# Fewer semaphore waits, and the shifted rows by a second TensorE transpose, in a Mamba layer with six local-attention layers

## The reference, cut to what matters

```python
# Mamba, forward and flipped, on the normalised x
h = h * exp(dt * A) + (dt * u) * B;  y = (h @ C + u * D) * silu(z)

# each of the 6 layers; shift_tokens moves half of the features one token on
q, k, v = split(shift_tokens(x) @ Wqkv)          # 16 heads of 64
q, k = rotary(l2norm(q) * qs), rotary(l2norm(k) * ks)
k2, v2 = [previous window of 32, own window of 32]
out = softmax(mask(q @ k2.T * 8)) @ v2
x = out @ Wo + x
x = (a * gelu(gate)) @ W2 + b2 + x                # a, gate = layernorm(shift_tokens(x)) @ W1 + b1
```

## Time and profile before

| what | us |
|---|---|
| median of 2 runs | 3917.16 |
| lowest and highest of them | 3916.18, 3918.15 |
| the profiled execution, its own time | 3923.24 |
| its span, first to last instruction | 3921.5 |
| outside the span | 1.7 |

### The profile page before, as it was taken

The page is one execution under the profiler, slowest core; times in us unless marked ns, Lnnn a source line. Parts: engine busy times, 40 slices in busy tenths (PEclk is TensorE's granted clock), DMA queues, the critical chain, the costliest instruction groups (busy, mean ns, idle before and its releaser), DMA issues.

```text
span 3921.5 us, 115027 instructions
## 1 busy us (share of the span) xinstructions
PE 3716.7 (95%) x45104; PEld 2578.1 (66%) x45104; DVE 3307.3 (84%) x3327; ACT 3035.4 (77%) x7250; POOL 3178.6 (81%) x2370
## 2 busy tenths in 40 slices
PE   7999999988799999999999999999999999999997
PEld 2444444433377777777777777777777777777775
DVE  2999999999688887888878887888878888788885
ACT  7776667666488887888878887888878887888885
POOL 2787778877688888888888888888888888888883
PEclk8999999999899999999999999999999999999999
DMA  1122222222100000000000000000000000000001
GB/s 60 71 81 76 76 74 73 81 73 84 43 21 7 20 7 6 21 7 20 7 10 18 7 20 6 11 17 7 21 6 10 18 7 20 7 11 6 7 7 47
DMA packets 62307, 115.01 MB, mean 29 GB/s; under 512 B 10820, under 2 KB 37320, under 8 KB 61648
## 3 DMA queue, kind: packets, MB, share of 16 engines
q1 hardware_dynamic: 61776, 107.66, 8.3%
HBM read 90.32 MB, written 4.72 MB: 24 GB/s over the span
## 4 chain that ended last, share of the span: by engine, by line
PE 66%; issue 3%; ACT 2%; POOL 1%; DVE 0%; POOLq 0%; ACTq 0%; DVEq 0%
PE ps L1199 17%; PE ps L1127 13%; PE ps L1188 9%; PE ps L1138 8%; PE ps L1175 6%; PE ps L1224 5%; PE ps L1237 3%; PE ps L1160 2%; PE ps L1206 1%; PE ps L1212 1%; PE ps L1146 1%; POOL resid L1604 1%; POOL resid L1626 0%; ACT prob L1329 0%; ACT mixed L1338 0%
## 5 line engine op out<-in xcount | busy, mean ns | idle before, releaser
L1604 POOL TENSOR_TENSOR resid<-resid,sq 128x1024 f32<-128x1024 f32 x384 | 910.3, 2376 | 2.1 <-DVE sq L1459 2.1
L696 POOL TENSOR_TENSOR read<-state,c_row 128x1024 f32<-128x1024 f32 x256 | 646.2, 2540 | 178.7 <-DVE state L658 99.4
L1626 POOL TENSOR_TENSOR resid<-resid,rnorm 128x1024 f32<-128x1024 f32 x384 | 725.0, 1904 | 17.8
L1199 PEld LDWEIGHTS ps<-mixed,w_vo 128*128 128x128 f32 x6144 | 710.9, 193 | 26.7 <-issue 18.6
L1199 PE MATMUL ps<-mixed,w_vo 128*128 128x128 f32 x6144 | 720.2, 276 | 3.2 <-ACT mixed L1338 3.2
L1127 PE MATMUL ps<-w_qk,xs_parts 128*128 128x512 f32 x2304 | 635.6, 412 | 37.4 <-issue 19.4
L1329 ACT ACTIVATE prob<-ps,stat 128x64 f32<-128x64 f32 x3072 | 650.8, 382 | 0.7 <-DVE stat L1479 0.5
L1459 DVE TENSOR_TENSOR sq<-ps,rope_l 128x1024 f32<-128x1024 f32 x384 | 462.5, 1205 | 103.9 <-ACT sq L1291 103.7
L1472 DVE TENSOR_TENSOR resid<-ps,rope_l 128x1024 f32<-128x1024 f32 x384 | 464.9, 1211 | 82.5 <-ACT sq L1291 75.2
L1291 ACT ACTIVATE sq<-ps 128x1024 f32<-128x1024 f32 x384 | 395.6, 1030 | 154.2 <-PE ps L1127 121.4
L1127 PEld LDWEIGHTS ps<-w_qk,xs_parts 128*128 128x128 f32 x2304 | 414.0, 192 | 152.5 <-issue 74.1
(11 more groups left out here) (149 smaller groups left out, 6038.1 us busy)
## 6 DMA issues: line engine op xcount, KB each, us to landing
c_row<-c_rows SPq DMA_DIRECT2D x128, 512.0 KB, 3.6
rows_back<-rows SPq DMA_DIRECT2D x192, 48.0 KB, 1.9
w_stage<-w_qk_hbm SPq DMA_DIRECT2D x12, 512.0 KB, 4.6
vo_stage<-w_v_hbm SPq DMA_DIRECT2D x6, 512.0 KB, 4.0
vo_stage<-w_o_hbm SPq DMA_DIRECT2D x6, 512.0 KB, 5.0
rows_back<-rows SPq DMA_DIRECT2D x192, 16.0 KB, 1.8
xn<-x_hbm SPq DMA_DIRECT2D x4, 512.0 KB, 5.7
kept<-resid SPq DMA_DIRECT2D x8, 256.0 KB, 4.2
```

What stands on the lines that cost most here:

```text
L696: pool.tensor_tensor(read[:, h, g % 2, :], state[:, h, g % 2, :], c_row[:, g % C_AHEAD, :], ALU.mult).then_inc(done[f"rd{h}"], 1)
L1199: last = pe.matmul(bank[:, 0:P], w_vo[:, l % 2, head_at(place_h), :], mixed[:, odd, place_h, :], start=place_h == 0, stop=place_h == HEADS ...
L1604: pool.tensor_tensor(qk[:, tile % 2, cols], qk[:, tile % 2, cols], sq[:, 1 + part, :], ALU.add).then_inc(done[f"rotated{part}"], 1)
L1626: pool.tensor_tensor(heads, heads, norms, ALU.mult).then_inc(done[f"normed{part}"], 1)
```

## The change

Two things are changed.

1. `after` sorts the stages asked for by the engine that makes them (`places` numbers the stages of each engine's order). Of each engine's only the latest is waited for, and only when the waiting engine hasn't already waited for that stage or a later one of that engine (`latest`, with the record `met`). Stages with a negative number are left out. Bank waits and stage waits of a stage go through one such call (`freed_by`). `add_ff` and `in_norm` are now stages like others (`x_of`), so that `x_low` isn't waited for any more. In `mamba` the waits for `cd` and `cst` (transfers) stay as they were, and are asked for first.
2. `rows_back` and its two transfers a tile are gone. `row_turn` makes two transposes, one of the tile's 128 columns of xa and one of the 128 columns that begin 32 before, into the two quarters of one bank; `copy_rows` copies 128x256 instead of 128x128 into `rows[:, tile % 2, back or own, :]`. `mix` takes both from there.

```diff
+def places(orders):
+    return {stage: (side, n) for side, order in enumerate(orders) for n, stage in enumerate(order)}
+
+def latest(met, eng, stages, places):
+    asked = {}
+    for side, n, stage in sorted((*places[stage], stage) for stage in stages if stage[1] >= 0):
+        asked[side] = n, stage
+    asked = {side: x for side, x in asked.items() if x[0] > met.get((eng.engine, side), -1)}
+    met.update({(eng.engine, side): n for side, (n, _) in asked.items()})
+    return [stage for _, stage in asked.values()]

# mamba
             for name, k in producers:
-                if k >= 0:
+                if k >= 0 and name in ("cd", "cst"):
                     eng.wait_ge(c_spread[k % C_AHEAD] if name == "cd" else done[name], COUNT[name, k])
+            for stage in latest(met, eng, [x for x in producers if x[0] not in ("cd", "cst")], stands):
+                eng.wait_ge(done[stage[0]], COUNT[stage])

# transformer
-    rows = sb("rows", [P, 2, P])
-    rows_back = sb("rows_back", [P, 2, P])
+    rows = sb("rows", [P, 2, 2, P])

     def after(eng, *producers):
-        for name, k in producers:
-            eng.wait_ge(done[name], k + 1)
+        for name, k in latest(met, eng, producers, stands):
+            eng.wait_ge(done[name], k + 1 + CHUNKS * int(name == "add_ff"))

             for tile in range(ALL_TILES):
                 l, t, odd = place(tile)
-                shift_rows(tile)
+                after(sp, ("copy_rows", tile))

             def row_turn(tile):
                 l, t, odd = place(tile)
-                ff_added(pe, CHUNKS * l + t // CHUNK_TILES)
-                bank = turn_free("row_turn", tile)
-                pe.transpose(bank[:, 0:P], shifted(xa, t * P, P), ident[:, :]).then_inc(done["row_turn"], 1)
+                bank = turn_free("row_turn", tile, x_of(CHUNKS * l + t // CHUNK_TILES))
+                first = column(t * P)
+                for back in (WINDOW, 0):
+                    to = bank[:, 0:P] if back else bank[:, P:2 * P]
+                    last = pe.transpose(to, xa[:, first - back:first - back + P], ident[:, :])
+                last.then_inc(done["row_turn"], 1)

             def mix(tile):
-                after(pe, ("turn_probs", tile), ("copy_rows", tile))
-                shifted_back(pe, tile)
-                banks = [turn_free("mix", tile, w) for w in range(WINDOWS)]
-                for own, of in enumerate((rows_back, rows)):
+                after(pe, ("turn_probs", tile), ("copy_rows", tile), *[x for w in range(WINDOWS) for x in freed_by("mix", tile, w)])
+                banks = [turn_bank("mix", tile, w) for w in range(WINDOWS)]
+                for own in range(2):

             def copy_rows(tile):
-                after(act, ("row_turn", tile))
-                if tile >= 2:
-                    after(act, ("mix", tile - 2))
-                    shifted_back(act, tile - 1)
-                act.copy(rows[:, tile % 2, :], turn_bank("row_turn", tile)[:, 0:P]).then_inc(done["copy_rows"], 1)
+                after(act, ("row_turn", tile), ("mix", tile - 2))
+                act.copy(rows[:, tile % 2, :, :], turn_bank("row_turn", tile)[:, 0:2 * P].rearrange(
+                    "p (b n) -> p b n", b=2)).then_inc(done["copy_rows"], 1)
```

More of the change, by code:

```diff
@@ L204, in mamba @@
         y_ps = [ps[:, 4 + 2 * h:6 + 2 * h, :] for h in range(HALVES)]
+        met, stands = {}, places((PE_SEQ, ACT_SEQ, DVE_SEQ, POOL_SEQ))
         COUNT, done = {}, {}
@@ L970, in transformer, with x_of @@
     KEPT = 16 * CHUNKS
+    met, stands = {}, places((PE_SEQ, ACT_SEQ, DVE_SEQ, POOL_SEQ))
+    done |= {"in_norm": x_ready, "add_ff": x_ready}
     def after(eng, *producers):
-        for name, k in producers:
-            eng.wait_ge(done[name], k + 1)
-    def ff_added(eng, chunk):
-        eng.wait_ge(x_low, chunk + 1)
-        eng.wait_ge(x_ready, chunk + 1)
-    def shifted_back(eng, tile):
-        eng.wait_ge(rows_shifted[tile % 2], 32 * (tile // 2 + 1))
+        for name, k in latest(met, eng, producers, stands):
+            eng.wait_ge(done[name], k + 1 + CHUNKS * int(name == "add_ff"))
+    def x_of(chunk):
+        return ("in_norm", chunk) if chunk < CHUNKS else ("add_ff", chunk - CHUNKS)
     def indexed(name, f, n):
@@ L1028, in load_w2 @@
                 if l >= 2:
-                    ff_added(sp, CHUNKS * l - 1)
+                    after(sp, x_of(CHUNKS * l - 1))
                 sp.dma_start(w2[:, l % 2], hbm["w2"][l]).then_inc(w2_loaded, 16)
                 sp.dma_start(lp[:, l % 2], hbm["lp"][l]).then_inc(w2_loaded, 16)
-            def shift_rows(tile):
-                l, t, odd = place(tile)
-                after(sp, ("copy_rows", tile))
-                if tile >= 2:
-                    after(sp, ("mix", tile - 2))
-                before = (tile - 1 if t % SEQ_TILES else tile) % 2
-                sp.dma_start(rows_back[WINDOW:P, odd], rows[0:P - WINDOW, odd]).then_inc(rows_shifted[odd], 16)
-                sp.dma_start(rows_back[0:WINDOW, odd], rows[P - WINDOW:P, before]).then_inc(rows_shifted[odd], 16)
             load_heads(0)
@@ L1096, in turn_free @@
                 elif last:
-                    after(pe, (TURN_READERS[last[0]], last[1]))
-                return turn_bank(name, k, i)
+                    return [(TURN_READERS[last[0]], last[1])]
+                return []
+            def turn_free(name, k, *producers):
+                after(pe, *producers, *freed_by(name, k))
+                return turn_bank(name, k)
             def fold(two):
@@ L1103, in stage @@
                     pe.wait_ge(wvo_loaded, 32 * l + 32)
-                    banks = [turn_free(f"fold{two}", l, odd) for odd in range(2)]
+                    after(pe, *freed_by(f"fold{two}", l, 0), *freed_by(f"fold{two}", l, 1))
+                    banks = [turn_bank(f"fold{two}", l, odd) for odd in range(2)]
                     for h in range(8 * two, 8 * two + 8):
@@ L1114, in stage @@
                     l, t, odd = place(tile)
-                    after(pe, ("rest", tile))
                     if t == 0:
@@ L1118, in stage @@
                     if tile == 0:
-                        pe.wait_ge(x_ready, 2)
-                    if part:
-                        after(pe, ("cosines0", tile), ("sines0", tile))
-                    elif tile:
-                        after(pe, ("cosines1", tile - 1), ("sines1", tile - 1))
+                        after(pe, ("in_norm", 1))
+                    other = tile if part else tile - 1
+                    after(pe, ("rest", tile), (f"cosines{1 - part}", other), (f"sines{1 - part}", other))
                     for c in range(2):
@@ L1193, in output @@
                 l, t, odd = place(tile)
-                after(pe, *[(f"copy_mixed{w}", tile) for w in range(WINDOWS)])
                 if t == 0:
                     pe.wait_ge(vo_copied, 4 * l + 4)
-                bank = turn_free("output", tile)
+                bank = turn_free("output", tile, *[(f"copy_mixed{w}", tile) for w in range(WINDOWS)])
                 for place_h in range(HEADS):
@@ L1230, in ff_output @@
             def ff_output(chunk):
-                after(pe, *[(f"product{k}", chunk) for k in range(3)])
                 l = chunk // CHUNKS
@@ L1234, in ff_output @@
                     pe.wait_ge(w2_loaded, 32 * l + 32)
-                bank = turn_free("ff_output", chunk)
+                bank = turn_free("ff_output", chunk, *[(f"product{k}", chunk) for k in range(3)])
                 for k, (lo, m) in enumerate(HIDDEN_PARTS):
@@ L1334, in stage @@
                 def stage(tile):
-                    after(act, ("mix", tile))
-                    if tile >= 2:
-                        after(act, ("output", tile - 2))
+                    after(act, ("mix", tile), ("output", tile - 2))
                     act.copy(mixed[:, tile % 2, :, w * WINDOW:(w + 1) * WINDOW], turn_bank("mix", tile, w).rearrange(
@@ L1364, in round_chunk @@
             def round_chunk(chunk):
-                after(act, ("affine", chunk))
-                if chunk:
-                    after(act, *[(f"{name}{k}", chunk - 1) for name in ("gate", "value") for k in range(3)])
+                after(act, ("affine", chunk), *[(f"{name}{k}", chunk - 1) for name in ("gate", "value") for k in range(3)])
                 act.copy(ff_parts[:, 0, :], xc[:, :]).then_inc(done["round_high"], 1)
@@ L1492, in turn_probs @@
             def turn_probs(tile):
-                after(dve, ("normalise_probs", tile))
-                if tile >= 2:
-                    after(dve, ("mix", tile - 2))
+                after(dve, ("normalise_probs", tile), ("mix", tile - 2))
                 dve.transpose(prob_t[:, tile % 2].rearrange("p h o n -> p (h o n)"),
```

88 lines of the change are left out of this document (27 added, 61 removed).

## The result

The kernel after the change takes 3888.64 us (median of 2 runs, 3887.85 to 3889.42), against 3917.16: a ratio of 0.9929, with an interval of 0.9905 to 0.9953. I had forecast 3920 with a range from 3900 to 3942. It is 28.5 us faster instead of 3 us slower, and outside the range. The profiled execution is the one of 3887.85 us, its span 3886.0, 35.4 us under the profiled one of before.

A forecast was written before the change was run, and what follows sets the result against it. It took VectorE in the Mamba part and TensorE in the transformer as the limits. Terms -4, -1, +15.7, -2.4, -5 and zeros summed to +3.3 us; from 3917.16 this gave 3920, range 3900 to 3942.

The forecast's parts named there:

- What bounds the kernel: VectorE full at 97 to 98% in Mamba, TensorE at 97.4% in the transformer, about 75 us idle there.
- The second transpose and its absorption: 192 more on TensorE: 144 at 0.109 us, +15.7; 48 at row_turn(1) absorbed by a wait for ScalarE, -2.4 us.
- ScalarE's copy: Row copy grows from 128x128 to 128x256, 279 to 384 ns, on an engine idle 17%: 0 us.
- The transfers: Two a tile removed from SyncE's queue; no wait of TensorE names a DMA: 0 us.
- The other engines' waits: Fewer waits on ScalarE, VectorE and GpSimd, hidden since these engines are idle 15% and more: 0 us.
- The late waits: Waits ending late, largest for the folded weights, more often carried by the instruction itself: -1 us, bounds -4 and 0.
- The score-to-mix step: TensorE, once a chunk: 1.48 us falls to 1.39 if semaphores cause the difference, 48 x 0.09: -4 us, or 0.
- The issue time: TensorE's instruction blocks: 8 or 9 fewer, -1, and earlier border crossings, -4: -5 us, bounds -15 and +12.
- the sequencer is the hidden limit: Rival: a third of TensorE's 131 us removed semaphore time is on the path, -44 + 16 = -28: 3889; chance 0.14.
- Transposes in full: Rival: TensorE pays all 192 in the transformer, nothing comes back, +21 to +31 us: 3938 to 3948; chance 0.15.
- The clock: Rival: added transposes lower the transformer's mean granted clock from 0.99 to 0.97, +57 us: 3977; chance 0.02.
- The Mamba part: VectorE stays full there, GpSimd's read_out asks in another order: 0 us, bounds -5 and +5.

The follow-up runs named there:

- turn_only: Kernel before with the second row transpose and without the transfers, all other waits asked as before: 3936.05 us, ratio 1.0047.
- waits_only: Kernel after with the transfers and single row transpose of before, so only the waits are shortened: 3878.57 us, ratio 0.9897.
- pe_waits_only: Kernel after with only TensorE's waits shortened, the other engines asking for all stages again: 3894.8 us, ratio 0.994.
- mix_all: Kernel after with TensorE's mix alone asking for every producer again, 431 semaphore instructions more: 3899.18 us, ratio 0.996.
- mamba_all: Kernel after with the Mamba part's waits as before the change, the transformer as after: 3878.95 us, ratio 0.9903.

## Why the prediction was wrong

**What bounds the kernel: right.** VectorE in the Mamba part, TensorE in the transformer, and the gain stays within the 75 us of idle time.

**The second transpose and its absorption: right.** Forecast +15.7 - 2.4 = +13.3, the table gives +20.2 - 6.7 = +13.5, from 109 ns for each of the 192. At row_turn(1) row transpose to projection went from 1.100 to 1.067 us by the medians (forecast 1.05). The Trainium skill's 275 ns for a transpose ("TensorE: Matmul & The Clock Gate", Part 4: PE-mode transpose) would have made 53 us of it; `turn_only` shows 18. The absorption has a catch that I had not priced: in `waits_only` the first of these head turns has shrunk from 551 to 464 ns by itself (medians), so the shortened waits had already freed a part of the slack that the transpose moves into. Against `waits_only` the transposes cost 20.8 us, with 4.0 back there. I had also said that TensorE would be busy some 20 us longer; in the transformer it is 3.1. The lengths of matmuls are modelled, so what came back in the head turns (6.7), in the step to `mix` (4.3) and a part of the holes (32.4 us start to start, 25.3 by the waits) had stood as busy time before.

**ScalarE's copy: right**, 388 ns against 384. **The transfers: right**, nothing on the path. **The other engines' waits: right** in the transformer; the 6 us between `pe_waits_only` and after lie ahead of it. **The late waits: right**, 13.1 to 12.2 us in front of the head turns.

**The score-to-mix step: right**, 48 x 0.090 = 4.3 us against 4, and by `mix_all` it is the semaphores' and not the change of shape.

**The issue time: here it failed**, the term of -5 with bounds -15 and +12. In its place the table has -36: the 36.1 of the `score` steps and the 4.1 behind them, less the 4.3 of the step just named. Gaps inside `score` fell by 32.4 us start to start, and `mix` behind them by 4.1. I had the parts in hand: the blocks of 256, `score` as the stage that empties them fastest, 43 stops with 30.8 us. The step that went wrong is "8 or 9 blocks fewer, 2.3% of 50.2 us: -1", with 4 more for a sequencer that isn't held up. It prices the stops by the number of borders, but what counts is how far ahead the sequencer is when it reaches them: the packet ahead of a late border started at +0.77 us in before and at -0.41 in after, and the holes there fell from 41 of 51 to 16 of 46. The borders' number fell by 10 of 366. And the sentence before it, "In most places none, as rows 3 show", judged that lead from chunks without a stop. They prove that the array isn't slowed where the lead lasts. They say nothing of where it doesn't. Also, 19.4 of those 50.2 us were not issue time at all.

The rival "the sequencer is the hidden limit" gave 3889 and this is what came, but by luck: its third of 131 us, spread over small holes hidden in TensorE's busy time, is not what happened. Most of the gain is in holes that were large, few, in the open and all in one stage. "Transposes in full" comes near in `turn_only`, which is the change without its first half: 3936, where the rival gave 3938 to 3948. But it too is not what happened: the `row_turn` steps of `turn_only` cost 20.7 us and 6.2 came back behind row_turn(1), the absorption that this rival denies. The clock did not fall: 0.978 in the profiled run with 192 more transposes, 0.99 to 1.00 in the windows.

**The Mamba part**: forecast 0 with bounds of 5; the profiles show 8.0 us less before the first `row_turn`, cause open. The Trainium skill ("Runtime: NRT & Kernel Launch", Instruction fetch mechanics) calls border crossings "mostly hidden". In this kernel three quarters of those in `score` are, and the rest were worth 31 us of idle time; the rule in its plain form pointed me to the small value.

**A version that beats both.** `waits_only` at 3878 us (0.9897, and 0.99 when it was run again) takes the shortened waits and leaves rows to the transfers, which nothing waited for. TensorE, the full engine, should not have been given the work. `mamba_all` is as fast, 3879, by what I read as the position of its borders, and I would not build on that: any later edit ahead of the transformer moves them again.

## What to carry to other kernels

A wait that is always met is free only while its engine's sequencer has a lead; look for the stage that spends this lead, a long run of short matmuls, and strip what stands in front of it first. Two such instructions a tile in front of `score` cost 31 us here, over four times as many elsewhere 13. Judge a stage by its mean over all its occurrences beside its median, not by one clean chunk: the `score` that `mix` follows had a median of 1.71 and a mean of 2.23 us, and half of the gain inside `score` (19.0 of 36.1 us) lay there. And split a change of two parts: this one's second half costs 10 to 18 us of what the first half earns.

## What the runs showed of the hardware

- A stop of up to 2.0 us in the middle of a stage with no wait in it, always at the same place modulo 256 of TensorE's instruction stream, and mostly (41 of 49 in before) where the previous border lies within 64 instructions ahead of a run of 256 that is emptied in 1.4 us. The matmul behind the stop starts 1.15 to 1.61 us after an instruction packet's end in all 369 cases.
- 128 met semaphore instructions in a row with nothing queued cost about 11 us (0.09 each), although each is recorded as lasting 51 ns; consecutive ones start about 110 ns apart.
- Two kernels with the same arithmetic on TensorE differ by 10 us (3889 and 3879), as I read it through the position of block borders, so a difference of 0.3% between two versions of this kernel may say nothing of either edit.
- A wait for GpSimd of 19.4 us stood as "issue" while a semaphore instruction carried it, and under its own name once the matmul carried it.
